# An order of pieces per engine, and other groupings of the rotation and the norm, in the last stage of a fused transformer kernel

## The chip, the cores and the metric

One Trainium2 chip, one core. The time is the device time of the whole program in microseconds (us). A core has five engines that run their own instruction queues and meet at semaphores: TensorE (PE; its weight loads are shown as PEld), VectorE (DVE), ScalarE (ACT), GpSimd (POOL) and SyncE (SP, which here issues the DMAs).

## The reference, cut to what matters

The program runs two blocks of attention with feed-forward and a cross attention (stages a to c, not touched here), and then, as stage d, a transformer of DEPTH = 6 layers over x of shape (2, 512, 128). One layer of stage d:

```python
# attention: 16 heads of 64, window of 32 tokens, each window sees itself and the one before
q, k, v = split(shift_tokens(x) @ Wqkv)            # 128 -> 3 * 1024
q, k = l2norm(q) * q_scale, l2norm(k) * k_scale    # per head: t / max(norm(t), 1e-12)
q = q * cos * scale + rotate_half(q) * sin * scale # the same for k with 1 / scale
x = softmax(8 * q @ k.T, masked) @ v @ Wo + x
# feed-forward
xn = layernorm(shift_tokens(x)) * g + b
a, gate = split(xn @ W1 + b1)                      # 128 -> 2 * 341
x = a * gelu(gate) @ W2 + b2 + x
```

`rotate_half` swaps the two halves of the 64 numbers of a head and changes the sign of one; the signs are in the table. All of it is float32.

## The kernel before

**Tiles and chunks.** The 1024 tokens are NT = 8 tiles of 128 tokens, TB = 4 tiles to a batch. For a tile, the projection of queries and keys is four chunks of 512 columns, c = 0, 1 (queries) and 2, 3 (keys), eight heads each. A chunk k = 4 n + c of tile n goes through five engines, all in the piece `proj`:

- PE multiplies into the PSUM bank PM[0] (L1325), and for c = 0 and 2 also a part of the values into PM[1] (L1336). In the same piece it transposes the chunk of the same c of the tile before, from QR into PX (L144).
- ACT copies PM[0] to RAW (L1487), copies the transposed chunk from PX to QT or KT (L1492), squares RAW into SQ (L1496), and copies values (L1501).
- DVE makes RAW times cosine table, R1 (L1567), and the two halves of RAW times sine table, R2 (L1568 and L1569), then the sums of squares per head (`tensor_reduce`, L1571, 128x512 to 128x8), then the floor of 1e-24 (L1573, 128x8, into RN).
- POOL adds R1 and R2 into QR (L1279, called the join here), raises the eight sums to the power -0.5 (L1281, called the power), and for keys multiplies QR by them (L1285). For queries the factor is applied to the scores, on DVE in L1579.
- RAW, SQ, R1, R2 and SS have two buffers, QR has four. So L1567 of chunk k waits for the join of chunk k - 2 (for keys, in this version, for their multiplication), and POOL's join of chunk k waits until PE has transposed chunk k - 4.

**Pieces of the attention.** For tile n: `score` (PE L1347 and L1353; DVE L1579 scale, L1582 maximum, L1584 subtraction), `exp` (ACT L1504), `weigh` (DVE L1587 sum and L1589 reciprocal), `pturn` (PE transposes the weights, ACT copies them, L1508), `mix` (PE L1375 times values; DVE L1595 scales), `oturn` (PE transposes, ACT copies, L1512), `out` (PE L1395, DVE L1599 adds to Y).

**Pieces of the feed-forward,** once per batch: `f1a` (PE transposes Y, ACT writes the shifted XS), `f1b` (PE transposes back; DVE L1605 to L1613 statistics; POOL L1289 the power of 128x4 numbers; DVE L1616 normalizes), `f2` (transposed, ACT scales), `f3` three times (PE L1436 gate and L1438 a; ACT L1526 Gelu; DVE L1627 product), `f4` (PE L1444; DVE L1631 adds the bias, L1634 adds to Y). `shift`, at the start of a layer, makes XS from Y, and waits for `f4` of its batch in the layer before. PE's pieces `shift`, `out`, `f1a`, `f1b`, `f2` and `f4` share the PSUM bank PV, in the order in which they are issued.

**The order.** `layer_order` writes out one list of pieces for all engines. It is by steps: in step k an engine does the projection of tile k, the scores of tile k - 2 and the mixing and output of tile k - 3, and within a step each piece has a place (score 0, chunk c at 10 (c + 1), and the others between). A batch's feed-forward starts in the step TB (b + 1) + 3, that is step 7 for batch 0 and step 11 for batch 1. A loop over layers has a period of 9 steps, so that steps 9 to 12 of a layer fall together with steps 0 to 3 of the next; step 8 has no projection of its own. Each engine runs the pieces of this list that it has a part in, in the order of the list. `Bank` and `Event` turn places in the order into semaphore counts.

Of the kernel before, what the change touches and what calls it, by code (L numbers as in the profile page):

```python
# [1032 lines left out]
def layer_order():  # L1033

    forward = {(0, 0): [("f1a", None)], (0, 1): [("f1b", None)], (1, 0): [("f2", None)],
               (1, 1): [("f3", 0)], (1, 2): [("f3", 1), ("f3", 2)], (1, 3): [("f4", None)]}
    order = []  # L1040
    for k in range(NT + 5):
        s, o = k - 2, k - 3
        if k == PERIOD:
            order.append((k, -5, "early", None))
        if 0 <= s < NT:
            order.append((k, 0, "score", s))
        if 1 <= k <= NT:
            order.append((k, 5, "vin", k - 1))
        if k in (0, TB):
            order.append((k, 1, "shift", k // TB))  # L1050
        for c in range(4):
            at = 10 * (c + 1)
            if k <= NT:
                order.append((k, at, "proj", (k, c)))
            if c == 0 and 0 <= o < NT:
                order.append((k, at + -1, "pturn", o))
            if c == 1 and 0 <= s < NT:
                order.append((k, at + 1, "exp", s))
            if c == 2 and 0 <= s < NT:
                order.append((k, at + 3, "weigh", s))  # L1060
            if c in (1, 2) and 0 <= o < NT:
                order.append((k, at + 4, ("mix", "oturn")[c - 1], o))
            if c == 3 and 0 <= o < NT:
                order.append((k, at + 5, "out", o))
            for b in range(B):
                for name, x in forward.get((k - TB * (b + 1) - 3, c), []):
                    order.append((k, at + (1 if name in ("f1a", "f2") else 6), name, b if x is None else 3 * b + x))
        if k < NT:
            order.append((k, 48, "vout", k))
        if k == NT + 2:  # L1070
            order.append((k, 49, "output", None))
        if k == NT + 4:
            order.append((k, 49, "late", None))
    return order

# [673 lines left out]
```

## Time and profile before

| | us |
|---|---|
| median of 3 runs | 2322.05 (2320.69 to 2334.29) |
| profiled execution | 2328.08 |
| its span, from first to last instruction | 2326.2 |
| stage d in it, from the first projection on | about 1226 to 2326 |

Busy over the span: PE 1867.0 us (80%), DVE 1716.5 (74%), ACT 1279.5 (55%), POOL 906.5 (39%). TensorE's mean granted clock is 0.919 of full speed. Stage d starts at about slice 21 of the page's 40; in it the DVE row stands at 7 to 9 tenths, PE at 6 to 8, POOL at 5 to 8, ACT at 4 to 6. A row of a timeline gives start, busy time, engine, line, operation and tiles, and in brackets how long the engine had been idle and what ended that. Successive instructions of an engine overlap a little, so what one costs its engine is read from start to start.

### The profile page before, as it was taken

The page shows a single profiled execution, that of the slowest core. Times are in us where ns is not written, and L with a number is a line of the kernel's source. Part 1 is how long each engine was busy: PE and PEld are TensorE (multiplying, and loading weights), DVE is VectorE, ACT ScalarE, POOL GpSimd, SP SyncE. Part 2 cuts the span into 40 slices and gives each one's busy share as a digit, 9 for nine tenths or more (in the row PEclk, how much of TensorE's full clock was granted, in tenths as well). Part 3 has the DMA queues.
Part 4 walks back from the last instruction along what each step waited for, and adds up shares of the span by engine and source line. Part 5 has one row for each costly group of instructions (what it writes and reads, how often), then busy time and mean ns, then how long its engine had stood idle before and what let it go on. Part 6 is the DMA issues. An engine that isn't in the chain of part 4 may idle for free. (4 is left out here: it accounts for less than half of the span.)

```text
span 2326.2 us, 52273 instructions
## 1 busy us (share of the span) xinstructions
PE 1867.0 (80%) x18512; PEld 924.7 (40%) x18512; DVE 1716.5 (74%) x3041; ACT 1279.5 (55%) x1850; POOL 906.5 (39%) x913
## 2 busy tenths in 40 slices
PE   5745888888888888888846887887888888788786
PEld 3531222222222222222223654654655555555564
DVE  4744677767777777777648988878878887887893
ACT  4411665656666666666635655645546555555553
POOL 0012111111111111111028858648657666675670
PEclk9955898989999999999958998999999999999998
DMA  1002223232222232222004323323323333232330
GB/s 34 1 24 61 46 56 61 56 59 55 59 55 59 55 59 55 59 55 57 2 30 119 92 85 92 87 85 92 94 87 92 86 93 92 68 111 75 84 84 10
DMA packets 88745, 152.83 MB, mean 66 GB/s; under 512 B 16819, under 2 KB 51669, under 8 KB 84693
## 3 DMA queue, kind: packets, MB, share of 16 engines
q1 hardware_dynamic: 86421, 149.04, 26.2%
q8 instruction: 136, 2.23, 0.4%
q10 hardware_dynamic: 2112, 0.94, 0.2%
q14 instruction: 76, 0.62, 0.1%
HBM read 98.03 MB, written 51.12 MB: 64 GB/s over the span
## 5 line engine op out<-in xcount | busy, mean ns | idle before, releaser
L899 DVE TENSOR_REDUCE ENM<-PM 128x1 f32<-128x512 f32 x1024 | 658.4, 685 | 257.2 <-PE PM L722 248.8
L819 ACT ACTIVATE EPT<-PA 128x1024 f32<-128x1024 f32 x512 | 512.4, 1021 | 220.2 <-PE PA L734 137.6
L722 PE MATMUL PM<-EKX,EQX 48*128 48x512 bf16 x1024 | 356.3, 402 | 104.3 <-DVE ENM L899 84.0
L1279 POOL TENSOR_TENSOR DQR<-DR 128x512 f32<-128x512 f32 x192 | 245.4, 1278 | 289.0 <-DVE DR L1569 289.0
L1281 POOL TENSOR_TENSOR DRN<-DRN,DHALF 128x8 f32<-128x8 f32 x192 | 354.8, 1848 | 8.4
L642 POOL CAST ENMP<-ENM 128x16 bf16<-128x16 f32 x64 | 12.6, 196 | 786.2 <-DVE ENM L899 786.2
L744 PE MATMUL PV<-EPT,EVP 128*32 128x512 f32 x2048 | 286.7, 633 | 0.8 <-ACT EPT L819 0.7
L734 PE MATMUL PA<-EQX,EKX 51*128 51x512 bf16 x1024 | 254.8, 397 | 28.4 <-DMA EQX<-EROWS 15.9
L722 PEld LDWEIGHTS PM<-EKX,EQX 48*128 48x128 bf16 x1024 | 85.8, 95 | 482.1 <-DVE ENM L899 392.7
L1325 PE MATMUL PM<-DWQKV,DXS 128*128 128x512 f32 x384 | 218.0, 651 | 47.3 <-ACT XNT L1526 29.2
L1487 ACT ACTIVATE DRAW<-PM 128x512 f32<-128x512 f32 x192 | 114.7, 598 | 143.4 <-PE PM L1325 106.4
L1567 DVE TENSOR_TENSOR DR<-DRAW,DTAB 128x512 f32<-128x512 f32 x192 | 146.6, 764 | 37.2 <-ACT DRAW L1487 15.9
L144 PE MATMUL PA<-IDENT,DP 128*128 128x128 f32 x768 | 116.7, 293 | 46.2 <-DVE DP L1595 37.3
L144 PEld LDWEIGHTS PX<-IDENT,DQR 128*128 128x128 f32 x768 | 99.7, 147 | 111.8 <-issue 107.8
L1571 DVE TENSOR_REDUCE DSS<-DSQ 128x8 f32<-128x512 f32 x192 | 129.5, 674 | 0.0
L144 PE MATMUL PX<-IDENT,DQR 128*128 128x128 f32 x768 | 121.3, 283 | 7.6 <-issue 6.9
L144 PEld LDWEIGHTS PA<-IDENT,DP 128*128 128x128 f32 x768 | 91.1, 149 | 89.6 <-DVE DP L1595 68.5
L1496 ACT ACTIVATE DSQ<-DRAW 128x512 f32<-128x512 f32 x192 | 121.7, 634 | 0.8
L1508 ACT ACTIVATE DPT<-PA 128x512 f32<-128x512 f32 x96 | 52.3, 597 | 115.3 <-PE PA L144 113.5
L1395 PE MATMUL PV<-DWO,DOT 128*128 128x128 f32 x768 | 100.2, 286 | 15.6 <-DVE XN L1616 12.6
L1285 POOL TENSOR_TENSOR DQR<-DQR,DRN 128x512 f32<-128x512 f32 x96 | 102.0, 1063 | 13.8
L1336 PE MATMUL PM<-DWQKV,DXS 128*128 128x512 f32 x192 | 103.3, 621 | 3.3 <-DVE DU L1627 3.3
(208 smaller groups left out, 2960.9 us busy)
## 6 DMA issues: line engine op xcount, KB each, us to landing
DV<-d_vpark SPq DMA_DIRECT2D x192, 256.0 KB, 5.0
d_vpark<-DVT SPq DMA_DIRECT2D x48, 512.0 KB, 2.6
e_park<-EPARTS SPq DMA_DIRECT2D x64, 192.0 KB, 2.9
EQX<-e_park SPq DMA_DIRECT2D x32, 384.0 KB, 5.5
EKX<-e_park SPq DMA_DIRECT2D x32, 384.0 KB, 9.2
DWQKV<-in_WqkvR SPq DMA_DIRECT2D x6, 1536.0 KB, 9.5
e_park<-EPARTS SPq DMA_DIRECT2D x64, 128.0 KB, 2.7
e_park<-EPARTS SPq DMA_DIRECT2D x64, 64.0 KB, 2.1
```

The costliest lines, as they stand in the source:

```text
L144: return pe.matmul(out, lhsT=in_, rhs=m.IDENT[0:k, 0:k], is_transpose=True, start=True, stop=True)
L722: pe.matmul(PM[:, r, :], lhsT=QX[64 * r:64 * r + KQ, b, hp, t * 128:(t + 1) * 128], rhs=KX[64 * r:64 * r + KQ, b, hp, :], start=True, stop ...
L734: mm = pe.matmul(PA[:, 2 * pair + r, :], lhsT=KX[64 * r:64 * r + KS, b, hp, kt * 128:(kt + 1) * 128], rhs=QX[64 * r:64 * r + KS, b, hp, :] ...
L744: mm = pe.matmul(PV[32 * j:32 * j + 32, :], lhsT=VP[:, g // HG, kt, 4 * (g % HG) + j, :], rhs=PT[:, kt, j * S:(j + 1) * S], start=kt == 0, ...
L819: s_.activation(PT[:, kt, pair * 2 * S:(pair + 1) * 2 * S], PA[:, 2 * pair:2 * pair + 2, :].rearrange("p a b -> p (a b)"), ACT.Exp, scale= ...
L899: v.tensor_reduce(NM[:, g % 2, t, j, 0:1], PM[:, r, :], AX.X, ALU.max, negate=True).then_inc(maxed, 1)
L1279: g.tensor_tensor(qr, r1, r2, ALU.add).then_inc(roped.sem if queries else joined.sem, 1)
L1281: g.tensor_tensor(rn, rn, HALF[:, 0:8], ALU.pow).then_inc(rooted.sem, 1)
L1325: pe.matmul(PM[:, 0, :], lhsT=XS[:, b, W + t * 128:W + (t + 1) * 128], rhs=WQKV[:, c * 512:(c + 1) * 512], start=True, stop=True).then_inc ...
L1496: s.activation(SQ[:, k % 2, :], RAW[:, k % 2, :], ACT.Square).then_inc(squared.sem, 1)
L1567: v.tensor_tensor(r1, x, bc(tab[:, 0], 1, [128, 8, DL]), ALU.mult).then_inc(step, 1)
L1571: v.tensor_reduce(SS[:, k % 2, :], SQ[:, k % 2, :].rearrange("p (h e) -> p h e", h=8), AX.X, ALU.add).then_inc(summed.sem, 1)
```

## The change

It changes stage d alone, in four ways.

1. Each engine gets an order of its own: `layer_order(engine)` reads places from tables. For DVE: `mix` comes right after chunk 0 and `weigh` ahead of chunk 1 (they were behind chunk 1 and chunk 2), and `f1b` is split, its normalization (`f1c`) coming behind chunk 2. For PE: `mix` ahead of chunk 1, `oturn` ahead of chunk 2, `score` at the end of a step instead of the start of the next and so ahead of `f4`, `f1a` behind chunk 1, `f2` at the end of step 7. For ACT: `exp` ahead of chunk 1, and in step 8 the first Gelu ahead of `exp`, the two others behind.
2. POOL: piece `proj` of chunk k does the join of k first and then what belongs to chunk k - 1: nothing for an even chunk; for an odd one a power of both chunks (128x16), and for keys the two multiplications. Order per tile: join 0; power, multiplication, multiplication of the tile before's keys; join 1; join 2; power of the queries; join 3. L1567 of chunk k now waits for the join of chunk k - 2 alone.
3. DVE: both halves of the sine product in one instruction (128x512, the halves read in reversed order).
4. DVE: the floor once per two chunks (128x16), after the odd one.

```diff
-def layer_order():
+TILE_PLACES = {
+    "score": {"tensor": (1, 47), "vector": (2, 5)},
+    "exp": {"scalar": (2, 16)},
+    "weigh": {"vector": (2, 20)},
+    "pturn": {"tensor": (3, 3), "scalar": (3, 4)},
+    "mix": {"tensor": (3, 18), "vector": (3, 11)},
+    "oturn": {"tensor": (3, 23), "scalar": (3, 29)},
+    "out": {"tensor": (3, 43), "vector": (3, 45)},
+}
+BATCH_PLACES = {
+    ("shift", None): {"tensor": (0, 1), "scalar": (0, 1), "gpsimd": (0, 1)},
+    ("f1a", None): {"tensor": (7, 22), "scalar": (7, 27)},
+    ("f1b", None): {"tensor": (7, 28), "vector": (7, 22), "gpsimd": (7, 26)},
+    ("f1c", None): {"vector": (7, 34.5)},
+    ("f2", None): {"tensor": (7, 49), "scalar": (8, 0)},
+    ("f3", 0): {"tensor": (8, 17), "scalar": (8, 13)},
+    ("f3", 1): {"tensor": (8, 33), "scalar": (8, 33)},
+    ("f3", 2): {"tensor": (8, 38.5), "scalar": (8, 36.5)},
+    ("f3v", 0): {"vector": (8, 12)},
+    ("f3v", 1): {"vector": (8, 23)},
+    ("f3v", 2): {"vector": (8, 38.5)},
+    ("f4", None): {"tensor": (8, 49), "vector": (8, 47)},
+}
+SYNC_PLACES = {"vin": (1, 5), "vout": (0, 48)}
...
@@ gpsimd
+                def norm_keys(layer, k):
+                    n, c = divmod(k, 4)
+                    if c % 2 == 0:
+                        return
+                    rn = RN[:, n % 2, 8 * c - 8:8 * c + 8]
+                    pool.wait_ge(floored.sem, floored.at(layer, k // 2))
+                    g.tensor_tensor(rn, rn, HALF[:, :], ALU.pow).then_inc(rooted.sem, 1)
+                    for i in range(2 if c == 3 else 0):
+                        qr = QR[:, (k - 1 + i) % 4, :].rearrange("p (h e) -> p h e", h=8)
...
+                        g.tensor_tensor(qr, qr, bc(rn[:, 8 * i:8 * i + 8], 2, [128, 8, DL]), ALU.mult).then_inc(roped.sem, 1)
...
-                    elif name == "proj" and n[0] < NT:
+                    elif name == "proj":
                         k = 4 * n[0] + n[1]
...
+                        if k < 4 * NT:
+                            pool.wait_ge(rotated.sem, rotated.at(layer, k))
+                            pool.wait_ge(turned.sem, turned.at(layer, k - 4))
+                            g.tensor_tensor(QR[:, k % 4, :], R1[:, k % 2, :], R2[:, k % 2, :], ALU.add).then_inc(joined.sem, 1)
+                        if 0 < k <= 4 * NT:
+                            norm_keys(layer, k - 1)
@@ tensor
-                            wait(roped, k - 4)
+                            if c < 2:
+                                wait(joined, k - 4)
+                            else:
+                                wait(roped, 2 * (n - 1) + c - 2)
@@ vector
-                        wait(roped, k - 2)
+                        wait(joined, k - 2)
                         v.tensor_tensor(r1, x, bc(tab[:, 0], 1, [128, 8, DL]), ALU.mult).then_inc(step, 1)
-                        v.tensor_tensor(r2[:, :, 0:32], x[:, :, 32:64], bc(tab[:, 1, 0:32], 1, [128, 8, 32]), ALU.mult).then_inc(step, 1)
-                        v.tensor_tensor(r2[:, :, 32:64], x[:, :, 0:32], bc(tab[:, 1, 32:64], 1, [128, 8, 32]), ALU.mult).then_inc(rotated.sem, 1)
+                        halves = lambda y: y.rearrange("p h (s e) -> p h s e", s=2)
+                        v.tensor_tensor(halves(r2), halves(x)[:, :, ::-1, :], bc(tab[:, 1].rearrange("p (s e) -> p s e", s=2), 1, [128, 8, 2, 32]),
+                                        ALU.mult).then_inc(rotated.sem, 1)
                         wait(squared, k)
-                        v.tensor_reduce(SS[:, k % 2, :], SQ[:, k % 2, :].rearrange("p (h e) -> p h e", h=8), AX.X, ALU.add).then_inc(summed.sem, 1)
-                        wait(summed, k)
-                        v.tensor_scalar(RN[:, n[0] % 2, 8 * c:8 * c + 8], SS[:, k % 2, :], 1e-24, None, ALU.max).then_inc(floored.sem, 1)
+                        v.tensor_reduce(SS[:, k // 2 % 2, 8 * (c % 2):8 * (c % 2) + 8], SQ[:, k % 2, :].rearrange("p (h e) -> p h e", h=8), AX.X, ALU.add).then_inc(summed.sem, 1)
+                        if c % 2:
+                            wait(summed, k)
+                            v.tensor_scalar(RN[:, n[0] % 2, 8 * c - 8:8 * c + 8], SS[:, k // 2 % 2, :], 1e-24, None, ALU.max).then_inc(floored.sem, 1)
```

## Rows read from the trace of the kernel before

**Rows 1.** Windows, fifth layer: each engine's busy us, granted clock, DMA share, GB/s.

```profile
1927.30:1959.70 32.40, 29.06 (x367) 19.41 (x366) 28.34 (x51) 21.18 (x36) 25.22 (x17) 0.94 0.25 74
1959.70:1982.20 22.50, 18.12 (x258) 11.06 (x257) 19.40 (x39) 14.30 (x27) 16.85 (x13) 1.00 0.51 132
1982.20:2008.40 26.20, 18.20 (x206) 11.06 (x205) 20.16 (x34) 9.59 (x15) 16.74 (x13) 0.87 0.06 21
2008.40:2024.90 16.50, 15.63 (x262) 11.15 (x261) 15.91 (x29) 12.74 (x22) 11.10 (x8) 1.00 0.61 149
2024.90:2042.10 17.20, 15.64 (x262) 11.15 (x261) 16.64 (x29) 11.04 (x20) 14.38 (x11) 1.00 0.49 128
...
2059.30:2084.80 25.50, 20.25 (x274) 14.34 (x275) 21.48 (x41) 13.13 (x24) 15.78 (x13) 0.87 0.43 119
2084.80:2108.40 23.60, 17.96 (x271) 12.71 (x270) 10.13 (x13) 7.72 (x11) 5.05 (x6) 0.93 0.09 31
```

**Rows 2.** Timeline of DVE, part of one step without feed-forward.

```profile
2029.38 0.68 DVE L1567 TENSOR_TENSOR DR<-DRAW,DTAB 128x512 f32<-128x512 f32 x1
2029.98 0.41 DVE L1568 TENSOR_TENSOR DR<-DRAW,DTAB 128x256 f32<-128x256 f32 x1
2030.32 0.41 DVE L1569 TENSOR_TENSOR DR<-DRAW,DTAB 128x256 f32<-128x256 f32 x1
2030.65 0.67 DVE L1571 TENSOR_REDUCE DSS<-DSQ 128x8 f32<-128x512 f32 x1
2031.36 0.74 DVE L1573 TENSOR_SCALAR DRN<-DSS 128x8 f32<-128x8 f32 x1
...
2033.30 0.68 DVE L1571 TENSOR_REDUCE DSS<-DSQ 128x8 f32<-128x512 f32 x1
2034.01 0.17 DVE L1573 TENSOR_SCALAR DRN<-DSS 128x8 f32<-128x8 f32 x1
2034.10 1.29 DVE L1595 TENSOR_TENSOR DP<-PA,DREC 128x512 f32<-128x512 f32 x2
...
2044.58 2.06 DVE L1584 TENSOR_TENSOR DP<-DP,DMAX 128x1024 f32<-128x1024 f32 x1
```

**Rows 3.** Timeline of POOL in the same step: a join and a power.

```profile
2030.81 1.27 POOL L1279 TENSOR_TENSOR DQR<-DR 128x512 f32<-128x512 f32 x1 [2.43 <-DVE DR L1569]
...
2038.70 1.65 POOL L1281 TENSOR_TENSOR DRN<-DRN,DHALF 128x8 f32<-128x8 f32 x1
```

**Rows 4.** Timeline of POOL elsewhere: a multiplication of keys.

```profile
1979.20 1.05 POOL L1285 TENSOR_TENSOR DQR<-DQR,DRN 128x512 f32<-128x512 f32 x1
```

**Rows 5.** Timeline of DVE at the same moment.

```profile
1979.27 1.27 DVE L1568 TENSOR_TENSOR DR<-DRAW,DTAB 128x256 f32<-128x256 f32 x1
```

**Rows 6.** Groups by line from 1100 us on: busy, mean ns | idle before, releasers.

```profile
L1281 POOL TENSOR_TENSOR DRN<-DRN,DHALF 128x8 f32<-128x8 f32 x192 | 354.8, 1848 | 8.4
...
L1573 DVE TENSOR_SCALAR DRN<-DSS 128x8 f32<-128x8 f32 x192 | 93.2, 486 | 6.6
...
L1504 ACT ACT_TABLE_LOAD x12 | 15.4, 1283 | 0.2
...
L1289 POOL TENSOR_TENSOR RSTD<-STD,DHALF 128x4 f32<-128x4 f32 x12 | 12.0, 1003 | 39.2 <-DVE STD L1613 39.2
```

**Rows 7.** Waits of DVE in stage d: us in total, times, longest.

```profile
DVE DP L1579 <- PE PA L1353: 42.7, 23, 6.5
...
DVE XN L1616 <- POOL RSTD L1289: 19.5, 12, 2.3
DVE DR L1567 <- ACT DRAW L1487: 15.9, 19, 1.5
```

**Rows 8.** Timeline of PE: the end of a feed-forward and scores behind it.

```profile
2003.44 2.94 PE L1444 MATMUL PV<-DW,DU 128*128 128x128 f32 x24 [1.50 <-DVE Y L1599]
2006.22 0.60 PE L1347 MATMUL PA<-DBAND,DEYE 128*128 128x512 bf16 x2
2006.75 1.48 PE L1353 MATMUL PA<-DKT,DQT 64*32 64x64 f32 x128
```

More of the change, by code:

```diff
@@ L1030 @@
 PERIOD = NT + 1
-def layer_order():
-    forward = {(0, 0): [("f1a", None)], (0, 1): [("f1b", None)], (1, 0): [("f2", None)],
-               (1, 1): [("f3", 0)], (1, 2): [("f3", 1), ("f3", 2)], (1, 3): [("f4", None)]}
-    order = []
[L1041 to L1073, printed above, removed]
-    return order
@@ new lines, with layer_order @@
+SYNC_PLACES = {"vin": (1, 5), "vout": (0, 48)}
+def layer_order(engine):
+    order = []
+    for n in range(NT):
+        for name, places in TILE_PLACES.items():
+            if engine in places:
+                order.append((n + places[engine][0], places[engine][1], name, n))
+        if engine == "sync":
+            for name, (k, at) in SYNC_PLACES.items():
+                order.append((n + k, at, name, n))
+    for b in range(B):
+        for (name, c), places in BATCH_PLACES.items():
+            if engine in places:
+                order.append((TB * b + places[engine][0], places[engine][1], name, b if c is None else 3 * b + c))
+    if engine == "sync":
+        order += [(PERIOD, -5, "early", None), (NT + 2, 49, "output", None), (NT + 4, 49, "late", None)]
+    else:
+        for k in range(NT + 1):
+            for c in range(4):
+                order.append((k, 10 * (c + 1), "proj", (k, c)))
+    return order
@@ L1084, with first_part, last_part, body_part @@
+def first_part(engine):
+    return [(0, name, n) for k, at, name, n in sorted(layer_order(engine), key=lambda x: x[:2]) if k < PERIOD]
+def last_part(engine):
+    return [(1, name, n) for k, at, name, n in sorted(layer_order(engine), key=lambda x: x[:2]) if k >= PERIOD]
+def body_part(engine):
+    return [(k // PERIOD, name, n) for k, at, name, n in sorted(layer_order(engine), key=lambda x: (x[0] % PERIOD, x[1], -x[0]))]
 class Bank:
@@ L1089, in __init__ @@
         self.filled, self.drained = filled, drained
-        self.first, self.body, self.last = ([(back, u) for back, name, n in order for u in uses(name, n)] for order in (FIRST, BODY, LAST))
+        self.first, self.body, self.last = ([(back, u) for back, name, n in order for u in uses(name, n)] for order in (first_part("tensor"), body_part("tensor"), last_part("tensor")))
     def number(self, layer, use_):
@@ L1241, in _ @@
                 sp.wait_ge(zeroed, 32)
-                for back, name, n in FIRST:
+                for back, name, n in first_part("sync"):
                     piece(0, name, n, None)
```

67 lines of the change are left out of this document (27 added, 40 removed).

## The prediction

> **What bounds the kernel now.** I read the windows first, cut from one score to the next. A layer takes 181 us, and in it DVE is the busiest engine wherever a projection runs: 16.6 of 17.2 us in a step without feed-forward, and the other engines have 1.5 us or more to spare [rows 1]. Two such steps are alike at 17.2, one takes 16.5. The remaining time is in the four stretches with feed-forward: 32.4, 22.5, 26.2 and 25.5, and 23.6 for step 8 with its loop end. Then the waits of DVE: it waits for scores from PE (42.7 us, longest 6.5, this at the loop end), for the reciprocal root of the layer norm (19.5) and for RAW (15.9) [rows 7].
>
> Then the timeline, for what a busy DVE does. From start to start, 512 columns cost 0.60 us; the two halves of the sine product cost 0.34 and 0.33 [rows 2]. L1573, eight columns, lasts 0.17 us once and 0.74 at another time. The second began at 2031.36, inside a join on POOL from 2030.81 to 2032.08, and ended with it [rows 2, 3]. The mean over 192 is 486 ns [rows 6], so 0.32 x 192 = 61 us of DVE go there. L1568 does the same beside a key multiplication: 1.27 us instead of 0.41, begun 0.07 behind it [rows 2, 4, 5]. L1584 takes 2.06 where 1024 columns should take 1.2 (twice 0.60). L1571 and L1595 hold to their times beside joins and powers. So DVE is bound, but some 2.0 us of a 17.2 us step (0.57 twice, 0.84 once) is standing still behind POOL. These are the instructions with both inputs in SBUF, and the small one. The Trainium skill, SBUF — State Buffer, Who interferes with whom, states this as an exclusive lock: a DVE instruction with two SBUF inputs, or in a two-port mode, and a GpSimd instruction that reads SBUF block each other for the whole instruction. These rows agree; it speaks against the new order, as worked out below.
>
> **The change, part by part.**
>
> *Sine product in one instruction.* 0.67 becomes 0.60: 0.07 x 192 = 13 us of DVE. The reversed order of two blocks is not in the trace. From below it could cost 0.60, as any 512 columns; from above twice that, 115 us in all, if blocks of 32 broke the stream. L1568 already reads blocks of 32 with gaps at full rate [rows 2], so I take 0.60.
>
> *Floor per pair.* L1571 to L1573 to the next start is 0.80 where a reduce alone would be 0.60 [rows 2]: 0.20 x 96 = 19 us less DVE. Its stall does not go with it: behind an even chunk the next instruction is now L1567, which needs the same interface as the join.
>
> *Power per pair.* 4 columns take 1.00 us, 8 take 1.65 [rows 3, 6]; 0.16 us a column on 0.35, so 16 should take 2.95. Bounds: 1.65 (columns free) and 3.3 (twice). POOL gains 0.35 per pair; what counts is where those 2.95 us lie.
>
> *A step without feed-forward, walked.* DVE work: 17.2 - 2.0 stalls - 4 x 0.07 - 2 x 0.20 = 14.5 us. Time 0 is the start of L1567 of chunk 0. Its sine product ends at 1.3; join 0 runs 1.4 to 2.6; power of the old keys 2.75 to 5.7; multiplications to 6.9 and 7.9; only then join 1. DVE meanwhile: mix 1.8 to 3.0, weigh to 4.4, chunk 1, whose floor at 6.4 stands until 6.9 (0.5). L1567 of chunk 2 stands until 7.9 (0.9). Join 1 has been waiting behind it and takes the interface from 8.4 to 9.7, so that the sine product of chunk 2 stands (1.1, as in rows 4 and 5). Join 2 starts at 10.3, L1567 of chunk 3 at 10.7 stands until 11.5 (0.8). Then the long power, out, and the score's 3.6 us, with join 3 under L1579 and L1582: no stall there, the 0.84 at L1584 goes. Stalls 3.3 for 2.0, and so 17.7 us. PE: its transposition of chunk 2 waits for the multiplication at 6.9, and some 11.5 us of its work lie from there to the next mix, which is ready at 18.4 and wanted at 19.5: hidden, with 1.1 us of cover. The three steps: 53.1 for 50.9, **+2.2** a layer.
>
> *Steps 0 and 1* (32.4): 1.4 us of work goes (eight sine products, four floors). In step 1 there is no weigh, so chunk 3's L1567 would wait for join 1, about as much as DVE now waits for key multiplications. **-1.6.**
>
> *Step 2* (22.5): 0.7 of work; with `f1c` behind chunk 2 the wait for the root (up to 2.3, rows 7) and 0.3 at its semaphore; stalls about 0.7 fewer, POOL having one pause. `f1b` on DVE waits for PE's `f1a` and `f1b`, which end under weigh and chunk 1. **-4.0.**
>
> *Step 7* (25.5): 0.7 of work, 1.6 for the root (19.5 / 12), and 1.9 of the waits for RAW, since PE and ACT do `f1a` no longer ahead of chunk 1. Against it, PE's `out` must wait for `f1c` (shared bank PV), and then `out` and `score` are 3.9 us of PE against 2.6 of DVE: 1.3 back. **-2.9.**
>
> *Step 3* (26.2): PE's scores, 2.0 us [rows 8], now stand ahead of `f4`, so DVE's last addition waits 2.0 longer and the score behind it some 1.3 less. ACT changes between Exp and Gelu four times per batch, not twice: 11 x 2 more loads at 1.28 us [rows 6], 28 us of ACT, of which one per batch lies ahead of `weigh` or the second Gelu. Less the work removed: **+0.8.** ScalarE: Activation LUTs, Rules for kernel authors, in the Trainium skill says to do all of one table set before changing; its 2.7 us a load would make that 59 us of ACT, but the trace has 1.28 and decides.
>
> *Step 8 and the loop end:* the scores of tile 7 come before the loop's end, so the wait of 6.1 to 6.5 us for them [rows 7] goes. But what the next layer's first chunk waits for is `f4`, then `shift`, ACT and the projection. That chain wins about 3 us (scores and a pause of PE out of its middle) and loses 2.6 in two loads. **-0.5**, between -5.5 (loads hidden) and +1.
>
> *Sum.* 2.2 - 1.6 - 4.0 - 2.9 + 0.8 - 0.5 = -6.0 us a layer, five times: -30. The first layer's pipeline filling and the last one's tail I put at 0: longer plain steps there against one shorter `f1`. Span 2326.2 - 30 = 2296.2; with the 1.9 us around it 2298.1. The profiled execution (2328.1) lies 6.0 above the median, so **2292 us**.
>
> **Rivals.**
> - *Stalls stay at 2.0 a tile* while the work goes: each of 48 tiles gains another 1.3, 62 us, so 2230. For it: stalls hang on tenths of a microsecond, and mix and weigh now cover the power. Against: three of six POOL instructions meet a product in the walk. The lock rule named above, as a mechanism of its own, gives the forecast's 17.7; without it, it would be this case.
> - *All given back:* plain steps at 18.3 instead of 17.7 (29 us over 48 tiles), so 2321. For it: DVE has 0 to 1 us of room to PE everywhere and the Gelu loads may all lie on the path. Against: the root's wait surely goes.
> - *Slower: POOL's join 1.* It is now behind a long power and two multiplications, and L1567 of chunk 3 waits for it; behind that stand chunk 3, out and score. In the walk it ends at 9.7 and is wanted at 10.7. From 1.0 us of further delay each microsecond costs 48 us. A power of 5 us (2 more) gives 1.0 for the wait and 1.0 in stalls further up, near 2.0 x 48 = 96, so 2388; slower by over 1% needs 1.1 us per tile. Against: the two shorter powers lie on a line that gives 2.95, and twice 1.65 is 3.3.
>
> **How the numbers follow.** Forecast 0.42 (its own range 2272 to 2315), stalls as before 0.25, all given back 0.19, POOL's join 0.14. About 1% is what a measurement of this kernel can tell from none; the limits are 2299 and 2345. Of the forecast two thirds lie under 2299, so faster 0.28 + 0.25 = 0.53; same 0.14 + 0.19 = 0.33; slower 0.14. The range from 2228 to 2340 leaves out the far side of POOL's join and the best loop end.
>
> **What would show it.** Between scores in a plain step: 17.7 us, L1567 and the sine product with means near 1.1 and 0.9 us, the floor near 0.5; the power of 16 columns at 2.95. No wait for the root ahead of the normalization (L1616 before); step 2 near 18.5 us. Gelu and Exp loads near 23 each. `f4`'s addition waiting some 4 us for PE in step 3. Wrong if plain steps are at 16.5 or less (stalls not as walked), if DVE waits for the join by more than 1 us in each step, or if the sine product takes over 0.7 us alone.

## The result

| | us |
|---|---|
| before, median of 9 runs | 2326.79 (2320.69 to 2337.38) |
| after, median of 9 runs | 2310.58 (2299.91 to 2325.73) |
| ratio | 0.9934, 95% interval 0.991 to 0.9957 |
| profiled execution of after | 2325.73, its span 2323.9 |

The change saves 0.66%, some 15 us, where the forecast was 30. The profiled execution of after is the longest of its nine. Of that, 8.8 us lie ahead of stage d, whose first product starts at 1236.93 us in it, and at 1228.12 in the profile of before, with the same code up to there. In the runs below the same point lies between 1217 and 1241. So stage d is compared with itself, from its first product to the end: 1098.1 us before, 1087.0 after, 11.1 less.

The fifth layer of after, cut at the same places as [rows 1] (the stretch with the loop end stands first here; then steps 2, 3, three plain steps, step 7, step 8). Columns as there.

```profile
1928.40:1960.70 32.30, 27.80 (x355) 17.72 (x356) 25.73 (x39) 19.82 (x35) 21.92 (x13) 0.95 0.25 71
1960.70:1979.10 18.40, 12.38 (x181) 7.52 (x181) 17.40 (x33) 10.86 (x20) 13.21 (x8) 1.00 0.47 131
1979.10:2005.00 25.90, 22.14 (x282) 13.75 (x281) 19.46 (x27) 15.62 (x25) 14.74 (x10) 1.00 0.17 47
2005.00:2023.30 18.30, 16.48 (x267) 11.83 (x268) 16.99 (x22) 13.34 (x23) 12.24 (x7) 1.00 0.52 136
2023.30:2042.10 18.80, 15.96 (x249) 10.25 (x248) 15.19 (x23) 10.58 (x19) 15.68 (x10) 0.91 0.36 94
2042.10:2059.40 17.30, 15.08 (x256) 10.21 (x253) 16.16 (x23) 10.40 (x19) 12.28 (x8) 1.00 0.29 75
2059.40:2080.90 21.50, 17.62 (x263) 12.76 (x264) 17.61 (x36) 11.57 (x21) 18.28 (x12) 0.92 0.43 112
2080.90:2106.30 25.40, 19.61 (x293) 14.43 (x291) 10.65 (x13) 12.62 (x18) 5.60 (x7) 1.00 0.23 77
```

Two things show. In the last two plain steps DVE's busy time has gone from 16.6 of 17.2 us to 15.2 of 18.8 and 16.2 of 17.3: it is no longer the engine that never rests. And step 2 is 4.1 us shorter [rows 1] while step 8 is 1.8 longer.

One layer is a thin base, as it turned out. Here are the distances from score to score, in all layers with a loop around them (layers 2 to 5):

| | before, the four layers | after, the four layers | mean difference | forecast |
|---|---|---|---|---|
| step 2 | 22.1, 22.0, 21.6, 22.4 | 18.3, 18.3, 18.9, 18.3 | -3.6 | -4.0 |
| step 3 | 28.5, 28.5, 28.5, 26.3 | 26.0, 26.0, 26.4, 26.0 | -1.8 | +0.8 |
| plain steps, three | 50.8, 50.8, 50.9, 50.9 | 52.9, 54.3, 52.9, 54.3 | +2.8 | +2.2 |
| step 7 | 23.0, 23.0, 24.6, 25.5 | 19.8, 21.4, 21.4, 21.5 | -3.0 | -2.9 |
| step 8 | 23.1, 23.6, 23.7, 23.6 | 25.2, 25.4, 25.5, 25.5 | +1.9 | } -2.1 |
| loop end, steps 0, 1 | 33.4, 33.4, 32.5, 32.3 | 32.4, 32.4, 32.4, 32.3 | -0.5 | } together |
| layer | 180.9, 181.3, 181.7, 181.0 | 174.7, 177.9, 177.5, 177.9 | -4.2 | -6.0 |

The three plain steps do not change alike. Before, they take 16.4, 17.2 and 17.2 us; after, 18.3, 17.3 and 17.3, and in two of the layers 18.7 for one of the two last, at a lower clock. So what they lose at equal clock is lost in the first.

Beside these four layers (-16.9 us), the first layer takes 166.0 us for 161.1, its filling 27.7 for 26.6, and the last layer is as before (step 8 in it 21.3 for 18.3, the rest 3 us less). That makes the 11.

What has come in the place of the old waits shows in the list of waits of after (what waited, for what: us in total, times, longest):

```profile
PEld PX L144 <- POOL DQR L1287: 102.1, 42, 8.1
...
PE PX L144 <- POOL DQR L1287: 68.8, 31, 7.3
...
DVE Y L1658 <- PE PV L1465: 39.5, 12, 4.9
DVE DR L1588 <- ACT DRAW L1508: 23.9, 20, 2.3
...
DVE DSS L1593 <- ACT DSQ L1517: 22.5, 7, 3.7
DVE DP L1602 <- PE PA L1374: 22.4, 16, 2.4
...
DVE DR L1588 <- POOL DQR L1302: 7.3, 11, 0.9
...
DVE XN L1640 <- POOL RSTD L1307: 2.7, 6, 1.1
```

The wait for the root is nearly gone (2.7 us for the 19.5 of [rows 7]), and DVE waits less for scores (22.4 for 42.7; another 13.3 us ahead of the same instruction, 3.3 in each loop end, have no releaser that the profile names). New are the first two lines: TensorE waits for the multiplication of the keys. Its weight loads (PEld) stand for 102 us, 42 times, its matmuls (PE) for 68.8 us, 31 times. In before these were 3.9 us (7 times) and 0.8 us (0.54 and 0.22, both in the first layer). Where the waits for the multiplication are given below as one total, it is that of the weight loads.

The groups of stage d of after (out and in tiles and shapes, count, busy us, mean ns, idle time before them). [rows 6] has the groups of before.

```profile
L1282 POOL TENSOR_TENSOR DRN<-DRN,DHALF 128x16 f32<-128x16 f32 x96 | 292.6, 3048 | 0.0
L1590 DVE TENSOR_TENSOR DR<-DRAW,DTAB 128x512 f32<-128x512 f32 x192 | 164.0, 854 | 0.0
L1588 DVE TENSOR_TENSOR DR<-DRAW,DTAB 128x512 f32<-128x512 f32 x192 | 156.0, 812 | 43.5 <-ACT DRAW L1508 23.9 <-POOL DTAB L1295 7.5 <-POOL DQR L1302 7.3
L1607 DVE TENSOR_TENSOR DP<-DP,DMAX 128x1024 f32<-128x1024 f32 x48 | 61.0, 1272 | 1.6
L1596 DVE TENSOR_SCALAR DRN<-DSS 128x16 f32<-128x16 f32 x96 | 32.3, 336 | 3.3
```

The power of 16 columns takes 3.05 us in the mean and 2.90 at least, for a forecast of 2.95.

**The ring of a plain step.** The timeline of after from 2023 us on, in parts: start, busy time, and in brackets idle time and what ended it. DVE starts chunk 0 at 2026.98.

```profile
2027.58 0.68 DVE L1590 TENSOR_TENSOR DR<-DRAW,DTAB 128x512 f32<-128x512 f32 x1
...
2028.35 1.27 POOL L1302 TENSOR_TENSOR DQR<-DR 128x512 f32<-128x512 f32 x1 [2.98 <-DVE DR L1590]
2029.58 2.91 POOL L1282 TENSOR_TENSOR DRN<-DRN,DHALF 128x16 f32<-128x16 f32 x1
2032.62 2.57 POOL L1287 TENSOR_TENSOR DQR<-DQR,DRN 128x512 f32<-128x512 f32 x2
...
2033.72 0.66 PE L144 MATMUL PX<-IDENT,DQR 128*128 128x128 f32 x4 [2.09 <-POOL DQR L1287]
2034.21 1.54 PE L1357 MATMUL PM<-DWQKV,DXS 128*128 128x512 f32 x2
2035.56 1.91 PE L1343 MATMUL PM<-DWQKV,DXS 128*128 128x512 f32 x2
...
2037.58 0.60 ACT L1508 ACTIVATE DRAW<-PM 128x512 f32<-128x512 f32 x1 [1.19 <-PE PM L1343]
...
2038.21 0.69 DVE L1588 TENSOR_TENSOR DR<-DRAW,DTAB 128x512 f32<-128x512 f32 x1 [1.87 <-ACT DRAW L1508]
...
2042.06 1.23 DVE L1602 TENSOR_TENSOR DP<-PA,DRN 128x1024 f32<-128x1024 f32 x1 [1.54 <-PE PA L1374]
```

The power of the old keys has had its floored sums since the end of the tile before, but it stands in POOL's queue behind join 0 of this tile, and that waits for DVE's product of chunk 0. So the way goes: DVE's start of chunk 0, product, join 0, power, multiplication, 6.7 us until PE may transpose (2026.98 to 2033.72). Behind this transposition PE has the values, chunk 3's projection, `out` and the scores, and then DVE has its three passes over them before it starts the next chunk 0. In the shorter step that follows, these are 6.9 us (transposition at 2052.46, score at 2059.4) and 3.7 us. 6.7 + 6.9 + 3.7 = 17.3. These three stretches follow one another by their starts, so they add up to the step whatever holds it; this way is called the ring below. That it would hold the step near this length alone is shown by e7 (17.1 us with nothing on DVE slow).

In this version it is not alone. Rows of DVE and PE from the same shorter step, which DVE starts at 2045.72:

```profile
2052.95 1.53 DVE L1590 TENSOR_TENSOR DR<-DRAW,DTAB 128x512 f32<-128x512 f32 x1
...
2055.71 1.68 DVE L1588 TENSOR_TENSOR DR<-DRAW,DTAB 128x512 f32<-128x512 f32 x1 [0.64 <-POOL DQR L1302]
...
2057.42 1.48 PE L1374 MATMUL PA<-DKT,DQT 64*32 64x64 f32 x128
...
2059.37 1.23 DVE L1602 TENSOR_TENSOR DP<-PA,DRN 128x1024 f32<-128x1024 f32 x1 [0.33 <-DVE Y L1622]
```

DVE stands for 0.85 and 1.0 us in its products and for 0.2 in the floor, 2.1 us in all, and waits 0.64 us for join 1, which stands behind the same power and multiplications in POOL's queue. With 14.7 us of bare work (e9) that is the step as well. The scores are done at 2058.90 and DVE's own work at 2059.04: two ways through the late power end together, the one over PE some 0.2 us ahead. The first of the three plain steps (18.3 us) is DVE's own: 2.8 us of standing still and 0.67 of waiting for `exp`, while PE's scores are done 1.1 us before DVE takes them.

In the step of 18.8 the ring runs at another clock, and there it is the longer way: DVE waits 1.87 us for RAW and 1.54 for the scores. The same three pieces of PE in the shorter step:

```profile
2052.46 0.66 PE L144 MATMUL PX<-IDENT,DQR 128*128 128x128 f32 x4 [2.10 <-POOL DQR L1287]
2052.95 1.02 PE L1357 MATMUL PM<-DWQKV,DXS 128*128 128x512 f32 x2
2053.82 1.02 PE L1343 MATMUL PM<-DWQKV,DXS 128*128 128x512 f32 x2
```

From the transposition's start to the end of chunk 3's projection it is 2.4 us here and 3.8 there, and the window's granted clock is 1.00 here and 0.91 there (1.2 of 2.4 GHz for a part of it). PE had stood for 2.1 us at the same wait in both, so this idle time alone doesn't bring the lower clock. It costs 1.4 us in one plain step of two of the four layers.

### The profile page after: what moved, and what is told of

The parts are those of the page before. It is cut to its first block and busy times, and to the rows that moved or that the text cites. A ratio compares the mean times of both kernels' runs of the same rounds, so it can differ in the third digit from the quotient of the medians.

```text
span 2323.9 us, 51831 instructions
## 1 busy us (share of the span) xinstructions
PE 1867.5 (80%) x18512; PEld 918.5 (40%) x18512; DVE 1671.1 (72%) x2753; ACT 1309.0 (56%) x1872; POOL 871.2 (37%) x817
## 3 DMA queue, kind: packets, MB, share of 16 engines
q1 hardware_dynamic: 86421, 149.04, 26.3%
## 5 line engine op out<-in xcount | busy, mean ns | idle before, releaser
L1302 POOL TENSOR_TENSOR DQR<-DR 128x512 f32<-128x512 f32 x192 | 256.4, 1341 | 311.2 <-DVE DR L1590 311.2
L1282 POOL TENSOR_TENSOR DRN<-DRN,DHALF 128x16 f32<-128x16 f32 x96 | 292.6, 3048 | 0.0
L734 PE MATMUL PA<-EQX,EKX 51*128 51x512 bf16 x1024 | 257.3, 400 | 29.0 <-DMA EQX<-EROWS 17.3
L1343 PE MATMUL PM<-DWQKV,DXS 128*128 128x512 f32 x384 | 217.4, 648 | 14.3 <-ACTq L1498 6.4
L1588 DVE TENSOR_TENSOR DR<-DRAW,DTAB 128x512 f32<-128x512 f32 x192 | 156.0, 812 | 43.5 <-ACT DRAW L1508 23.9
L144 PE MATMUL PX<-IDENT,DQR 128*128 128x128 f32 x768 | 125.0, 288 | 74.3 <-POOL DQR L1287 68.8
L1590 DVE TENSOR_TENSOR DR<-DRAW,DTAB 128x512 f32<-128x512 f32 x192 | 164.0, 854 | 0.0
L144 PE MATMUL PA<-IDENT,DP 128*128 128x128 f32 x768 | 106.7, 278 | 10.4 <-DVE DP L1618 7.2
L1287 POOL TENSOR_TENSOR DQR<-DQR,DRN 128x512 f32<-128x512 f32 x96 | 111.5, 1182 | 6.9
L1357 PE MATMUL PM<-DWQKV,DXS 128*128 128x512 f32 x192 | 110.1, 658 | 0.0
L1416 PEld LDWEIGHTS PV<-DWO,DOT 128*128 128x128 f32 x768 | 96.2, 203 | 19.3 <-DVE XN L1640 12.3
```

Source lines behind the costliest of these rows:

```text
L144: return pe.matmul(out, lhsT=in_, rhs=m.IDENT[0:k, 0:k], is_transpose=True, start=True, stop=True)
L734: mm = pe.matmul(PA[:, 2 * pair + r, :], lhsT=KX[64 * r:64 * r + KS, b, hp, kt * 128:(kt + 1) * 128], rhs=QX[64 * r:64 * r + KS, b, hp, :] ...
L1282: g.tensor_tensor(rn, rn, HALF[:, :], ALU.pow).then_inc(rooted.sem, 1)
L1302: g.tensor_tensor(QR[:, k % 4, :], R1[:, k % 2, :], R2[:, k % 2, :], ALU.add).then_inc(joined.sem, 1)
L1343: pe.matmul(PM[:, 0, :], lhsT=XS[:, b, W + t * 128:W + (t + 1) * 128], rhs=WQKV[:, c * 512:(c + 1) * 512], start=True, stop=True).then_inc ...
L1416: mm = pe.matmul(PV[:, 0:E], lhsT=OT[:, hp, :], rhs=WO[:, hp, :], start=hp == 0, stop=hp == HP - 1)
```

## The experiments

Each ratio is against the kernel before, run beside it on the same chip. "After" is 0.9934 (0.991 to 0.9957). The intervals of e5, e6, e8 and e12 overlap that one; what is said of their steps is read from the trace of one execution each.

**e1. The sine product alone.** Kernel before, with one instruction for both halves.

```diff
-v.tensor_tensor(r2[:, :, 0:32], x[:, :, 32:64], ...); v.tensor_tensor(r2[:, :, 32:64], x[:, :, 0:32], ...)
+v.tensor_tensor(halves(r2), halves(x)[:, :, ::-1, :], bc(...), ALU.mult).then_inc(rotated.sem, 1)
```

> The kernel before, with the sine product in one instruction and nothing else. If VectorE sets the pace of a plain step, its four saved 0.07 us come through: 17.2 us becomes 16.9, some 13 us in all (ratio to before 0.994). If GpSimd's joins, powers and multiplications set it, the stalls grow by what the work shrinks: plain steps stay at 17.2 and the ratio is 1.000. The instruction itself should last 0.68 us alone; near 1.2 would mean that the reversed blocks cost.

Measured: 2326.68 us, ratio 0.9971 (0.9942 to 0.9999). The new instruction takes 0.68 us, 0.60 from start to start, so blocks read in reversed order cost nothing. But a looped layer is 180.7 to 181.4 us for 180.9 to 181.7, and the plain steps take 51.3 together for 50.8 (17.9, 17.0, 16.4). The instruction's own 0.07 us are saved and the layer hardly gains. Saved DVE work becomes waiting elsewhere in the layer; which wait took it wasn't taken apart further.

**e2. The order alone.** After's places per engine; join, power, floor and multiplication per chunk and two sine halves, as in before.

```diff
-wait(joined, k - 2)
+wait(roped, k - 2)
-if 0 < k <= 4 * NT: norm_keys(layer, k - 1)
+(power of 8 columns and multiplication right behind each join, floor per chunk)
```

> The new orders per engine, with the joins, powers, floors and the two sine halves of the kernel before. Theory A (the gain is the order's): step 2 falls from 22.4 to about 19 us and step 7 by about 2, and the ratio to before is 0.990 or less. Theory B (order and grouping need each other): in the old grouping a key chunk keeps its power and multiplication ahead of the next join, so that VectorE, which reaches chunk 3 earlier, waits for it; the plain steps grow by 1 us or more and the ratio is 1.00 to 1.02.

Measured: 2350.1 us, ratio 1.0075 (1.0058 to 1.0093): slower. The three plain steps are 17.7, 18.7 and 18.3. DVE has hardly a wait in them (17.1 of 17.7 busy, 17.9 of 18.7) and stands in its instructions: the first sine half has a mean of 758 ns where it takes 410 undisturbed. Theory B has the ratio, but not by the wait that it names: DVE waits for these multiplications for 10.1 us in all.

```profile
L1580 DVE TENSOR_TENSOR DR<-DRAW,DTAB 128x256 f32<-128x256 f32 x192 | 145.6, 758 | 0.0
```

**e3. The grouping alone.** After, with the places of before's common order in its tables.

```diff
-    "score": {"tensor": (1, 47), "vector": (2, 5)},
-    "exp": {"scalar": (2, 16)},
+    "score": {"tensor": (2, 0), "vector": (2, 0)},
+    "exp": {"scalar": (2, 21)},
...
```

> The old common order, with the new grouping (joins ahead of powers, power and floor per pair, one sine product). Theory A: 5.6 us of VectorE work go from a layer, but the multiplication of keys comes behind the next tile's first join and a 3 us power, and TensorE waits for it; plain steps stay near 17 to 18 us and the ratio is 0.995 to 1.010. The rival (the grouping carries the gain) has plain steps at 16.5 and a ratio of 0.98 to 0.99.

Measured: 2379.04 us, ratio 1.0206 (1.0176 to 1.0236): slower still, and beyond both theories. The same wait as in after, but 1.7 times as long; a plain step of the fifth layer takes 20.2 us with DVE busy for 16.3 of them. The line of the waits, then the window:

```profile
PEld PX L144 <- POOL DQR L1287: 172.5, 47, 8.1
```

```profile
2066.80:2087.00 20.20, 16.37 (x256) 11.45 (x255) 16.32 (x22) 10.76 (x19) 13.87 (x8) 0.92 0.33 85
```

Each half of the change makes the kernel slower by itself (+0.75%, +2.1%), and both together make it 0.66% faster.

**e4. The power at once.** After, but POOL does power and multiplications right behind the join of the odd chunk, not behind the next even one's.

```diff
-                        if 0 < k <= 4 * NT:
-                            norm_keys(layer, k - 1)
+                            norm_keys(layer, k)
```

> The changed kernel, but GpSimd does power and multiplications in the piece of the odd chunk itself: join 0, join 1, power, join 2, join 3, power, multiplication, multiplication. If what gives the gain back is TensorE waiting for the key multiplication (102 us of weight loads waiting for it, and VectorE's wait of 3.6 us for the squares behind it), that wait goes: steps 0 and 1 fall from 28.7 by about 4 us, no plain step stays at 18.7, and the ratio to before is 0.975 to 0.985. If only the stalls at the shared interface count, the multiplications now meet the subtraction of the maximum (0.8 us a tile) and the ratio stays near 0.993 or rises.

Measured: 2286.45 us, ratio 0.9833 (0.9775 to 0.9891). The second plain step (the third takes 16.7 us too) and step 8, in the windows of the fifth layer:

```profile
1993.30:2010.00 16.70, 15.12 (x256) 10.46 (x255) 16.22 (x22) 10.96 (x21) 14.08 (x9) 1.00 0.41 110
...
2049.40:2073.90 24.50, 19.88 (x295) 14.74 (x293) 10.35 (x13) 13.38 (x19) 5.07 (x7) 1.00 0.17 67
```

PE's wait for the multiplication falls to 13.2 us, and DVE runs without a gap in this step, as in before. What it loses is now inside its instructions. Three of them in one step (timeline), and then the floor's group:

```profile
1997.53 1.53 DVE L1589 TENSOR_TENSOR DR<-DRAW,DTAB 128x512 f32<-128x512 f32 x1
...
2004.11 0.75 DVE L1595 TENSOR_SCALAR DRN<-DSS 128x16 f32<-128x16 f32 x1
...
2008.50 0.99 DVE L1595 TENSOR_SCALAR DRN<-DSS 128x16 f32<-128x16 f32 x1
```

```profile
L1595 DVE TENSOR_SCALAR DRN<-DSS 128x16 f32<-128x16 f32 x96 | 76.3, 795 | 3.3
```

The two floors end with joins on POOL (2003.56 to 2004.83, and the first of two from 2008.19 on), the product stands beside a key multiplication. 0.85 + 0.58 + 0.82 = 2.25 us of standing still on 14.5 us of work: 16.7. A step of after has 2.1 us of that too. What is gone here are PE's wait and DVE's wait for join 1, and both came from the late power and multiplications. Over all tiles e4 even stands still longer than after (2.2 us a tile for 1.5, counted as under e7) and is 1% faster. So the place of the power, not DVE's work or its stalls alone, was what held after; which of the two ways behind it, e7 tells. The move has a price: steps 2 and 7 take 19.5 and 22.7 to 23.5 us for 18.3 to 18.9 and 19.8 to 21.5 in after. Steps 0 and 1 with the loop end fall by 2.1 us (32.4 to 30.3), not by the 4 expected.

**e5. The first Gelu behind `exp`.** After, with half the table loads.

```diff
-    ("f3", 0): {"tensor": (8, 17), "scalar": (8, 13)},
+    ("f3", 0): {"tensor": (8, 17), "scalar": (8, 16.5)},
```

> The changed kernel, with ScalarE's first Gelu of a batch behind the Exp instead of ahead of it, so that the function tables are loaded twice a batch again (12 and 12 loads, not 23 and 23). If the extra loads lie on the path of steps 3 and 8, these shorten by up to 2.6 us each (26.0 and 25.5 now), 5 us a layer, ratio to before 0.983. If they are hidden, or the first Gelu is now late for VectorE's product, which stands ahead of the weighing there, nothing or a little is lost: 0.993 to 1.000.

Measured: 2302.89 us, ratio 0.9887 (0.9832 to 0.9941). Loads fall from 23 + 23 to 12 + 12. Step 3 takes 24.7 to 25.3 us (26.0 to 26.4 in after), step 8 24.3 to 24.5 (25.2 to 25.5): 1.0 us each, of 2.6 forecast at most. The stretch of the loop end gives 0.5 back (32.9 in the mean for 32.4), so a layer gains 1.4. The ratio lies between the two that were expected.

**e6. `f4` ahead of the scores on PE.**

```diff
-    ("f4", None): {"tensor": (8, 49), "vector": (8, 47)},
+    ("f4", None): {"tensor": (8, 46), "vector": (8, 47)},
```

> The changed kernel, with f4 ahead of the scores on TensorE again. VectorE's last addition then waits some 2 us instead of 4.9 (39.5 us in all now). If that wait is what lengthened step 8 by 1.9 us and holds the next layer's start, step 8 falls by 2 us, but the scores of tile 7 follow later by 2.9: the stretch from the score of tile 7 to the first product of the next layer grows. As a sum I expect within 1 us a layer of the changed kernel (ratio 0.993 plus or minus 0.003); the rival, that the addition's wait is pure loss, gives 0.983.

Measured: 2315.31 us, ratio 0.9946 (0.9917 to 0.9975), no gain over after. DVE's wait for `f4` falls from 39.5 to 22.0 us. Step 8 falls to 22.8, but the stretch behind it rises from 32.4 to 37.8: the scores of tile 7 are then late by more. A looped layer takes 179.2 us in the mean for 177.0, so this move of the change helps by the trace, though the ratio does not tell.

**e7. No shared interface.** After, with the joins and key multiplications on POOL replaced by powers of 6 and 4 columns, which last as long (means 1.336 and 1.14 us for 1.341 and 1.18) and read 6 and 4 columns in the place of 512. It leaves out the sum of the two products and the norm of the keys.

```diff
-g.tensor_tensor(QR[:, k % 4, :], R1[:, k % 2, :], R2[:, k % 2, :], ALU.add).then_inc(joined.sem, 1)
+g.tensor_tensor(QR[:, k % 4, 0:6], QR[:, k % 4, 0:6], HALF[:, 0:6], ALU.pow).then_inc(joined.sem, 1)
-g.tensor_tensor(qr, qr, bc(rn[:, 8 * i:8 * i + 8], 2, [128, 8, DL]), ALU.mult).then_inc(roped.sem, 1)
+g.tensor_tensor(qr[:, 0, 0:4], qr[:, 0, 0:4], HALF[:, 0:4], ALU.pow).then_inc(roped.sem, 1)
```

> The changed kernel, with each join (1.27 us) replaced by a power of 6 columns and each key multiplication (1.04 us) by a power of 4 columns, in place on QR, which is filled with ones at the start. It leaves out the sum of the two products and the norm of the keys. GpSimd is busy about as long and at the same places (1.33 and 1.00 us by 0.35 + 0.16 a column), but powers did not stop VectorE. If the stalls at the shared interface are the 2 to 3 us of a plain step, those fall from 17.3 to 14.5 to 15.5 us and the ratio to before to 0.94 or less. If VectorE's stalls are covered anyway because TensorE and ScalarE wait for GpSimd's multiplication, the plain steps stay above 16.5.

Measured: 2286.24 us, ratio 0.9811 (0.9763 to 0.9859). All stalls are gone. The means of the two products and the floor are now bare (groups), PE's wait for POOL stays (waits), and the last two plain steps still take 17.1 us (window; one of the eight in the looped layers, at a lower clock, 18.8):

```profile
L1589 DVE TENSOR_TENSOR DR<-DRAW,DTAB 128x512 f32<-128x512 f32 x192 | 132.2, 688 | 51.8 <-ACT DRAW L1509 40.0 <-POOL DTAB L1296 6.8 <-DVE XN L1641 2.9
L1591 DVE TENSOR_TENSOR DR<-DRAW,DTAB 128x512 f32<-128x512 f32 x192 | 131.7, 686 | 0.0
L1597 DVE TENSOR_SCALAR DRN<-DSS 128x16 f32<-128x16 f32 x96 | 16.8, 175 | 3.3
```

```profile
PEld PX L144 <- POOL DQR L1288: 96.0, 38, 7.6
```

```profile
1988.40:2005.50 17.10, 14.99 (x256) 10.36 (x255) 14.31 (x23) 10.40 (x19) 13.14 (x8) 1.00 0.35 95
```

With these bare means the stalls of the other kernels can be counted. After: (812 - 688) x 192 + (854 - 686) x 192 + (336 - 175) x 96 + (1272 - 1225) x 48 ns = 74 us, 1.5 us a tile. Before, from the same means and 0.41 us for a half [rows 2], 110 us, 2.3 a tile. In e7 DVE waits 40.0 us for RAW in the place of 23.9, and 1.2 us for the scores in each of these steps: here the ring alone holds them. Of the 4.9 us that a layer gains over after (172.1 in the mean for 177.0), the plain steps give 1.7; at equal clock it is 0.9 in the first of them (18.3 to 17.4) and 0.2 in each of the others. The rest lies in step 7 (1.1), at the loop end (1.6) and in step 2.

**e8. The power in two halves.** After, with two powers of 8 columns in the place of one of 16.

```diff
-g.tensor_tensor(rn, rn, HALF[:, :], ALU.pow).then_inc(rooted.sem, 1)
+g.tensor_tensor(rn[:, 0:8], rn[:, 0:8], HALF[:, 0:8], ALU.pow)
+g.tensor_tensor(rn[:, 8:16], rn[:, 8:16], HALF[:, 0:8], ALU.pow).then_inc(rooted.sem, 1)
```

> The changed kernel, with the power of a pair of chunks as two instructions of 8 columns instead of one of 16; the order stays. Two take 3.3 us and a gap for 2.9. If TensorE's wait for the key multiplication paces steps 0, 1 and some plain steps, each 0.4 us that it comes later comes through there: ratio to before 0.995 to 1.000. If it is covered, 0.993.

Measured: 2331.3 us, ratio 0.9989 (0.9952 to 1.0025). The two last 3.5 us in the mean instead of 3.05, and a plain step 17.6 instead of 17.3. PE's wait for the multiplication rises to 117.7 us. Of 0.45 us that only POOL spends, 0.3 go into each of the last two plain steps. Join 1 comes later with it too (DVE waits 12.5 us for joins, for 7.3), so this run shows that the late power paces these steps, and not by which of the two ways.

**e9. Both: the power at once and no shared interface** (the edits of e4 and e7; the same parts are left out).

> Power and multiplications in the odd chunk's own piece, and joins and key multiplications replaced by powers of 6 and 4 columns as in e7 (it leaves out the sum of the two products and the norm of the keys). There VectorE is busy without a gap in plain steps of 16.7 us, 2.2 of them stalls. If the shared interface paces a kernel only once TensorE no longer waits for GpSimd, these steps fall to 14.5 to 15.0 us now, where in e7 they fell by 0.2 only, and the ratio to before is 0.96 or less. If something else paces them, they stay above 16.

Measured: 2223.16 us, ratio 0.9545 (0.9496 to 0.9595). The third plain step (the second takes 14.8 us):

```profile
1955.50:1970.20 14.70, 14.70 (x255) 10.20 (x253) 14.08 (x23) 10.29 (x19) 13.20 (x9) 1.00 0.42 110
```

14.7 us, by the prediction's 14.5 of bare DVE work. In the last two plain steps the standing still behind POOL is worth 0.2 us as long as the ring holds (17.3 to 17.1, e7), and 2.0 once it is open (16.7 to 14.7). In the whole program e4 takes 1.0% of before from after, e7 1.2%, and both together 3.9%: two ways of nearly the same length hide each other, and one experiment on each shows little of what both are worth.

**e10. The power at once, and the first Gelu behind `exp`** (e4 and e5).

> Power and multiplications in the odd chunk's own piece, and the first Gelu behind the Exp. If the two gains lie in different stretches (plain steps and steps 0 to 2 the one, steps 3 and 8 the other), they add: 0.9833 times 0.9887 / 0.9934, ratio to before 0.979. If they overlap, 0.983.

Measured: 2276.01 us, ratio 0.9783 (0.9744 to 0.9821). This is the fastest version that computes everything: 50 us below before, 35 below after. Its interval overlaps e4's, but the sum is the one expected. A looped layer takes 171.9 to 173.1 us.

**e11. The power at once, in the old order** (e3's tables with e4's edit).

> Power and multiplications in the odd chunk's own piece, with the old common order of pieces. If the loss of e3 (ratio 1.021) was the late key multiplication alone, this is faster than before by most of the VectorE work saved: plain steps 16.5 to 17 and a ratio of 0.985 to 1.000. If the grouping as such costs in the old order, because the power of queries is late for the scores or the joins meet the products, it stays over 1.005.

Measured: 2331.99 us, ratio 1.0021 (0.9995 to 1.0046). The first product's mean is 966 ns for e4's 800, DVE waits 45.0 us for scores and 21.3 for the root again. The plain steps take 17.7 us in the mean. The ratio lies between the two that were expected, so the late multiplication was most of e3's loss and not all of it. The orders per engine are worth 1.9% with this grouping (1.0021 to 0.9833), and made the kernel 0.75% slower with the old one.

**e12. `f1b` and its normalization together.**

```diff
-    ("f1c", None): {"vector": (7, 34.5)},
+    ("f1c", None): {"vector": (7, 28)},
```

> The changed kernel, with the normalization f1c directly behind the statistics f1b on VectorE, ahead of chunk 2, as before the change. The wait for the reciprocal root then returns: GpSimd has to do a join and its two multiplications first, so 2.3 us or more in steps 2 and 7, 12 times. I expect step 2 at 21 to 22 us instead of 18.3 and a ratio to before of 1.005 to 1.015. If only TensorE's wait for the multiplication counts in these steps, it stays near 0.993.

Measured: 2315.95 us, ratio 0.9946 (0.9921 to 0.9971), not to be told from after, and not the loss of 1 to 2% over it that was expected. The wait is back in full:

```profile
DVE XN L1640 <- POOL RSTD L1307: 19.0, 12, 2.2
```

Step 2 takes 19.9 instead of 18.3 to 18.9, but step 7 20.6 instead of 21.4 (in three layers), and step 8 24.2 to 24.7 instead of 25.2 to 25.5. A wait of 19 us that comes back costs nothing that can be measured: DVE catches up in the steps behind, where others are the pace.

## Why the prediction was right and wrong

- **The plain steps: right size, half the reason.** Forecast 53.1 us, measured 52.9 in two layers and 54.3 in two. The walk got there with 3.3 us of stalls on 14.5 of work, the same in each step. Measured at full clock are 2.8 us of stalls and 0.67 of waiting for `exp` in the first, and 2.1 with 0.64 of waiting for join 1 in the others. **The failed step is this:** "some 11.5 us of its work lie from there to the next mix, which is ready at 18.4 and wanted at 19.5: hidden, with 1.1 us of cover". The walk's time for the multiplication was right, 6.9, measured 6.7. But it asked only for the next mix. Between the two PE's queue holds chunk 3's projection and the scores. The cover is 0.2 us there and not 1.1: without any stall the step is still 17.1 us (e7). RAW of chunk 3 comes at 9.8 us of the step (2055.55), when DVE has been free since 9.4; at the lower clock it comes at 11.2, and DVE stands for 1.9 us. What the late multiplication costs in all is read from e4: 3.1 us a looped layer (173.9 in the mean for 177.0), 1% of the program.
- **The same wait where the next tile is late.** A tile's keys are multiplied only behind the next tile's join 0, and nothing in the sum asked what that costs while the pipeline fills and at the loop's seam. PE waits there for 3.6 us in each looped layer, and in the first layer for 7.3, 3.4, 2.1, 1.0, 2.1 and 2.1 us (PE rows of the timeline), 18.0 in all; there DVE also waits for RAW for 1.9 to 2.2 us in each of three steps. "The first layer's pipeline filling and the last one's tail I put at 0" and "-1.6" for steps 0 and 1 are the terms: the first layer with its filling gave +6.0, and steps 0 and 1 with the loop end -0.5, where steps 0 and 1 alone were to give -1.6. With the power at once (e4) the first layer with its filling takes 183.7 us for 193.7 in after and 187.7 in before, and that stretch 30.3. Without the stalls (e7) it takes 184.2: here too the two ways are nearly equally long. These are single executions; e5, e6 and e12, with after's place of the power, have 189.6 to 191.6. The windows could have warned: in the first row of [rows 1] PE is busier (29.06 us) than DVE (28.34), where the prediction calls DVE the busiest engine wherever a projection runs.
- **Step 8 and the loop end**, forecast -0.5: with steps 0 and 1 it was +1.4 for -2.1, 3.5 us a layer and the largest miss in a looped layer. 2.1 of the loop end are the late power (e4: 32.4 to 30.3). The table loads are 1.0 of step 8, but 0.5 of that comes back behind it (e5). The scores ahead of `f4` cost step 8 some 2.6 us and save 5.4 behind it (e6), so their direction was right. Of DVE's wait of 6.1 to 6.5 us at the loop end, which was to go, 3.3 are left, and the profile names no releaser for them.
- **Step 3**, forecast +0.8, was -1.8. The row of 26.2 us was that of one layer; three others had 28.5. And "DVE's last addition waits 2.0 longer" was wrong for this step: it waits 2.1 us, for 2.2 before. [rows 8] had the reason: PE stood for 1.50 us ahead of `f4`, and the scores, now ahead of it, fall into that time. The longer wait is in step 8, where no term stood for it. Rows of after, and then the one of step 8 in before:

```profile
2004.01 0.69 DVE L1658 TENSOR_TENSOR Y<-Y,PV 128x512 f32<-128x512 f32 x1 [2.11 <-PE PV L1465]
...
2102.32 0.69 DVE L1658 TENSOR_TENSOR Y<-Y,PV 128x512 f32<-128x512 f32 x1 [4.87 <-PE PV L1465]
```

```profile
2101.28 0.69 DVE L1634 TENSOR_TENSOR Y<-Y,PV 128x512 f32<-128x512 f32 x1 [2.19 <-PE PV L1444]
```

In step 7 it was the other way round (25.5 in that layer, 23.0 in two), and "1.9 of the waits for RAW" came from there (1.2 and 0.7 us in that layer, none in the two of 23.0). Before's own four layers differ by 2 us in where they lose time, and by 0.8 in the sum.
- **Steps 2 and 7**, forecast -4.0 and -2.9, gave -3.6 and -3.0. The wait for the root went, as forecast (2.7 us left). But "1.6 for the root" in step 7 and up to 2.3 in step 2 were too much: 1.6 is the mean of 2.3 in step 2 and 1.1 in step 7, and with the wait back (e12), step 2 loses 1.4 of its 3.6, step 7 nothing, and the layer as a whole nothing. What made up the rest of the two gains was not taken apart.
- **Right:** the power, 2.95 forecast, 2.90 at least and 3.05 in the mean; the sine product, 0.60 from start to start; the loads, 23 each.
- **The rivals.** "All given back" (2321) had the right neighbourhood. Its condition, plain steps at 18.3, held in one of three, and its reason, "DVE has 0 to 1 us of room to PE everywhere", is near what happened, except that PE stood behind POOL. POOL's join 1 is a part, below the 1 us that was to be the sign: 0.64 us in each full-clock step of the last two, 7.3 us in all. "Stalls stay at 2.0": by the same count they fell from 2.3 to 1.5 a tile, and it brought little while the ring held. The Trainium skill's rule that was weighed there (SBUF — State Buffer, Who interferes with whom) holds for POOL's joins and multiplications: without them the products and the floor are bare (e7). It does not hold as stated for the powers, which read SBUF too, last 1 to 3 us and stop no product; there the measurement decides. For this change the rule was half of the answer.

The sum -6.0 a layer, five times, was -30. Measured in the profiled executions: four layers at -4.2, the first with its filling +6.0, the last 0, together -11. So of the 19 us that are missing, 12 lie in the first layer (2 to 4 fewer in e5, e6 and e12) and 7 in the four others.

## What to carry to other kernels

When pieces are moved in one engine's queue, follow the ring through all engines back to the moved piece and add it up; an engine that is 97% busy before is not the pace afterwards if the ring is longer than its work. Ask for every consumer behind the late piece in its queue, not only for the next use of its own result. Where two ways end within some tenths of a microsecond of each other, open each alone and then both. Take the terms from all repetitions of a loop, not from one.
